# A 64-state scan whose odd states hold the channels' halves exchanged: y summed in four 64x64 tiles, carries copied on GpSimd

## Chip, cores and metric

One NeuronCore of a Trainium2 chip runs the whole program. The metric is device time in microseconds (us), here of one core, lower is better. The time of the kernel before is the median of three runs, 10685.8 us (10685.3 to 10687.49).

## What is computed

Four layers in a row on x of shape (4, 128, 64, 64): a sparse attention, a selective scan with 64 states, a rank-one attention, and a two-way scan with 16 states. The change touches the second layer alone. Cut to what matters, with L = 4096 positions per sample and C = 128 channels:

```python
xproj = xp @ W_in
x_mamba, x_conv = split(xproj, 2, axis=-1)
xc = depthwise_conv3x3(x_conv) + b_conv;  xc = xc * silu(xc)
u = layernorm(x_mamba) * gamma + beta
A = -exp(A_log)                                  # (C, 64)
dtbc = u @ W_dt + b_dt                           # 8 + 64 + 64 columns: dt, B, C
delta = softplus(dt_raw @ W_dtr + b_dtr)         # (b, L, C)
deltaA = exp(delta[..., None] * A)               # (b, L, C, 64)
dBu = delta[..., None] * B_ssm[:, :, None, :] * u[..., None]
h[l] = deltaA[l] * h[l - 1] + dBu[l]             # along L, for each channel and state
y = einsum('bldn,bln->bld', h, C_ssm) + u * D_param
out = (y + xc) @ W_out
return x + out
```

## The kernel before

`scan_layer` (L455) keeps channels on the 128 partitions and positions on the free axis. The 4 x 4096 positions are cut into NCH = 16 chunks of CH = 1024, numbered K, four to a sample. In each chunk it goes through the 64 states as 32 pairs, k = 0 to 31; a state of a chunk is a unit, and P = 32 K + k counts pairs. Each engine runs its own program, written out by hand in the order of the pairs, and they meet in semaphores.

For one pair P with its units 2P (even) and 2P + 1 (odd):

- ScalarE: `decays` (L824) writes exp(A delta) of a unit into one of 4 buffers; `odd_input` (L832) writes the transposed input of the odd unit, eight 128x128 pieces scaled by B, into `xt` (L842). It also does the softplus (`soft_exp`, `soft_log`), the copies out of PSUM, and SiLU.
- TensorE: `turn_back` (L672) transposes `xt` into the two PSUM banks of the odd input. `broadcast_B` (L661) writes the row of B of the next pair's even unit to all partitions, into the two banks of the even input. `add_state` (L682) adds h C of one unit to `y_sum`, two banks in which all 64 states of a chunk are accumulated, by matmuls with the 128x128 identity (L688). Between them stand the taps of the 3x3 convolution (`CONV`, L710: k = 3, 7, 14 to 20 and 23 to 31) and the preparation of the next chunk (`prep_*`), and the output projection of the chunk before (`project`, k = 21 and 22).
- VectorE: `scan` (L1038) runs the recurrence of 1024 positions, L1049, for the even and then the odd unit; `even_input` (L1031) multiplies du by the broadcast B in PSUM, L1036; `keep` (L1052) copies the last column of each unit's h into `carry` (L1055), in the three of four chunks whose state is carried on. Extra work: `add_y` at k = 0 (L1023), `gate_conv` at k = 1 and 21 (L1017), `rstds` and `newton` at k = 4, `scale_u` at k = 5 and 6 (L1005), `bt_copy` at k = 13, `residual` at k = 21 and 22 (L1029).
- GpSimd: `product` (L948) multiplies h by the broadcast row of C, L951, into `hc`. Extra instructions: `squares` at k = 1, `add_conv` at k = 2, `split_rest` at 12, `split_last` at 15, `soft_low`, `soft_max`, `soft_sum`, `input_rate` at 18, 19, 20, 21.
- SP: `load_row` (L544) loads one row of C, 4 KB, to all partitions of one of CS = 5 buffers of `hc`, once `sum_mm` says that the unit five before has been added.

The order of TensorE's work around the change, for pair P (L711 to L742):

```python
turn_back(P)
if P:
    add_state(2 * P - 2)
...                      # convolution, preparation, projection
if P + 1 < NCH * PAIRS:
    broadcast_B(P + 1, p if k + 1 < PAIRS else 1 - p)
if P:
    add_state(2 * P - 1)
```

and of VectorE's: `scan(P, 0)`, `scan(P, 1)`, then `even_input(P + 1)`, then the two `keep`, then any extra work. An even scan waits until its buffer of h is free: until the product of the unit four before is done.

Of the kernel before, what the change touches and what calls it, by code (L numbers as in the profile page):

```python
# [454 lines left out]
def scan_layer(nc, x, w, sel, weights_in, conv_weights):  # L455
# [13 lines left out]
    with ctx:  # L469
# [12 lines left out]
        delta = sb("delta", [128, 2, CH])  # L482
        du = sb("du", [128, 2, CH])
# [7 lines left out]
        part = sb("part", [PARTS * SEL, CH], BF16)  # L491
        z1, z2 = sb("z1", [128, CH]), sb("z2", [128, CH])
        z3, rows_sb = usq, z1[0:S1, :]
        carry = sb("carry", [128, S1])
# [27 lines left out]
        c_in = [sem(f"c_in_{i}") for i in range(CS)]  # L522
        hc_done = sem("hc_done"); sum_mm = sem("sum_mm"); y_out = sem("y_out"); yg_ready = sem("yg_ready")
# [15 lines left out]
        def _(sp):  # L539
# [11 lines left out]

            sp.dma_start(conv_raw, conv_weights).then_inc(conv_in, 16)
            store_rows(0)
            for K in range(NCH):
                for q in range(S1):
                    load_row(K, q)
                    if q == 26 and K + 1 < NCH:
                        store_rows(K + 1)

        @block.tensor  # L560
        def _(pe):
# [120 lines left out]
            def add_state(unit):  # L682
                K, q = divmod(unit, S1)
                if q == 0:
                    at_least(pe, y_out, K)
                pe.wait_ge(hc_done, unit + 1)
                for j in range(2):
                    ins = nc.tensor.matmul(y_sum[:, half(j)], ident, hc[:, unit % CS, half(j)], start=q == 0,  # L688
                                           stop=q == S1 - 1)
                ins.then_inc(sum_mm, 1)  # L690
# [20 lines left out]
            for K in range(NCH):  # L711
                p = K % 2
                for k in range(PAIRS):
                    P = K * PAIRS + k
                    turn_back(P)
                    if P:
                        add_state(2 * P - 2)
# [19 lines left out]
                    if k in (21, 22) and K:  # L737
                        project(K - 1, k - 21)
                    if P + 1 < NCH * PAIRS:
                        broadcast_B(P + 1, p if k + 1 < PAIRS else 1 - p)  # L740
                    if P:
                        add_state(2 * P - 1)  # L742
            for unit in range(NCH * S1 - 2, NCH * S1):
                add_state(unit)
# [4 lines left out]
        def _(act):  # L749
# [25 lines left out]
            def split_high(K):  # L775
                act.wait_ge(bdt_out, 2 * K + 2)
                nc.scalar.activation(part[:], rest[0:PARTS * SEL, :], ACT.Identity,
                                     scale=w[0:PARTS * SEL, L1_AT["below_top"]][:, 0:1]).then_inc(part_ready, 1)

            def split_middle(K):  # L780
                act.wait_ge(rest_ready, K + 1)
                nc.scalar.activation(part[:], rest[0:PARTS * SEL, :], ACT.Identity,
# [22 lines left out]
            def soft_log(K):  # L805
# [3 lines left out]
                nc.scalar.activation(z3[:], z3[:], ACT.Identity, bias=wt("minus_one")).then_inc(exp_ln, 1)  # L809
                nc.scalar.activation(z2[:], z1[:], ACT.Ln, bias=1.0).then_inc(exp_ln, 1)  # L810

            def duT_copy(K, p, j):
                act.wait_ge(duT_mm, 2 * K + j + 1)
                nc.scalar.activation(duT[:, p, 4 * j:4 * j + 4, :].rearrange("p t d -> p (t d)"), prep_ps,
                                     ACT.Identity).then_inc(duT_out, 1)
# [94 lines left out]
        def _(pool):  # L910
# [5 lines left out]
            def split_rest(K):  # L916
                pool.wait_ge(part_ready, 2 * K + 1)
                own = rest[0:PARTS * SEL, :]
                nc.gpsimd.tensor_tensor(own, own, part[:], ALU.subtract).then_inc(rest_ready, 1)

            def split_last(K, p):
                pool.wait_ge(part_ready, 2 * K + 2)
                nc.gpsimd.tensor_tensor(stack[:, p, :], rest[0:PARTS * SEL, :], part[:],
# [63 lines left out]
        def _(dve):  # L987
# [64 lines left out]
            def keep(unit):  # L1052
                q = unit % S1
                dve.wait_ge(scan_done, unit + 1)
# [1112 lines left out]
```

## Time and profile before

| | us |
|---|---|
| median of 3 runs | 10685.8 |
| the profiled execution, its own time | 10684.37 |
| its span, first to last instruction | 10682.6 |
| granted clock of TensorE over the span | 0.987 |

A row of a group names the line, the engine (PE = TensorE matmul, PEld = its weight load, DVE = VectorE, ACT = ScalarE, POOL = GpSimd), the operation, the tiles written and read, the shapes and the count; then busy us and mean ns of one; then the engine's idle time before such instructions and who ended it. A row of a timeline has the start in us from the span's start, the length in us, and neighbours of one line merged (x4 is four records); in brackets the idle time before. An fp32 matmul leaves two records. The ends of matmul records are modelled, so steps between starts are the better measure. "128*64" is the array's share in use, rows by columns.

### The profile page before, as it was taken

The numbers are of one execution on the slowest core, as the hardware profiler recorded it, in microseconds if no ns is written. First come the engines' busy times: TensorE is split into PE (matmuls) and PEld (weight loads), VectorE is DVE, ScalarE is ACT, GpSimd is POOL, SyncE is SP. The second block draws the span as 40 slices with busy tenths as digits, with TensorE's granted clock in tenths as the row PEclk, the third lists the DMA queues.
The fourth block names the chain that finished last, engine by engine and source line by source line (L and its number), as shares of the span: only waits on it lengthen the run. The fifth ranks groups of instructions, "written<-read, shape, count | busy, mean of one in ns | idle before, by whom it ended". The sixth has DMA issues, their size and how long they took to land. (4 is left out here: it accounts for less than half of the span.)

```text
span 10682.6 us, 128608 instructions
## 1 busy us (share of the span) xinstructions
PE 10171.5 (95%) x41860; PEld 5735.0 (54%) x41860; DVE 8525.5 (80%) x8102; ACT 8064.2 (75%) x14637; POOL 5901.9 (55%) x2628
## 2 busy tenths in 40 slices
PE   9999999999899999999999999989999999999996
PEld 6767767677444444444444444444444444444442
DVE  7858768588599999999999311179999999999997
ACT  5646646466588888888888555589999998888885
POOL 0000000000388888888888200068888888888885
PEclk9999999999899999999999999999999999999998
DMA  1000000000245555555555100045545555455555
GB/s 40 0 1 0 0 0 0 0 0 0 74 175 173 177 175 173 175 176 174 174 174 179 39 8 8 8 146 173 170 168 170 169 171 173 170 176 174 170 176 213
DMA packets 325682, 1207.45 MB, mean 113 GB/s; under 512 B 36624, under 2 KB 36752, under 8 KB 321552
## 3 DMA queue, kind: packets, MB, share of 16 engines
q1 hardware_dynamic: 325232, 1201.95, 32.9%
q8 instruction: 222, 3.64, 0.1%
q14 instruction: 228, 1.87, 0.1%
HBM read 1145.18 MB, written 56.62 MB: 113 GB/s over the span
## 5 line engine op out<-in xcount | busy, mean ns | idle before, releaser
L1816 POOL TENSOR_TENSOR l_ring<-l_ring 128x1024 f32<-128x1024 f32 x1024 | 2425.9, 2394 | 427.3 <-DVE l_ring L1894 425.7
L951 POOL TENSOR_TENSOR l_hc<-l_h,l_hc 128x1024 f32<-128x1024 f32 x1024 | 2398.9, 2365 | 451.5 <-DVE l_h L1049 450.9
L1894 DVE TENSOR_TENSOR_SCAN l_ring<-l_ring,l_carry,l_ps 128x1024 f32<-128x1024 f32 x960 | 2199.2, 2332 | 0.9
L1525 PE MATMUL l_ps<-l_ring,w_sb 128*128 128x512 f32 x4096 | 1960.5, 601 | 106.3 <-POOL l_ring L1816 74.1
L688 PE MATMUL l_ps<-l_hc,w_sb 128*128 128x512 f32 x4096 | 1936.5, 595 | 69.0 <-POOL l_hc L951 61.6
L1049 DVE TENSOR_TENSOR_SCAN l_h<-l_decay,l_carry,l_ps 128x1024 f32<-128x1024 f32 x768 | 1760.0, 2333 | 4.3 <-issue 0.4
L116 POOL COPY l_qm<-l_q 128x128 f32 x128 | 82.9, 649 | 2574.4 <-PE l_ps L188 2178.3
L829 ACT ACTIVATE l_decay<-l_delta,w_sb 128x1024 f32<-128x1024 f32 x1024 | 1152.7, 1138 | 168.6 <-DVE l_h L1049 168.4
L1706 ACT ACTIVATE l_xt<-l_duT,l_BT 128x128 f32<-128x128 f32 x4096 | 1246.0, 388 | 0.0
L842 ACT ACTIVATE l_xt<-l_duT,l_BT 128x128 f32<-128x128 f32 x4096 | 1245.9, 387 | 0.0
L1693 ACT ACTIVATE l_ring<-l_delta,w_sb 128x1024 f32<-128x1024 f32 x1024 | 1163.0, 1139 | 48.8 <-DVE l_ring L1894 47.7
L1525 PEld LDWEIGHTS l_ps<-l_ring,w_sb 128*128 128x128 f32 x4096 | 738.2, 190 | 733.1 <-issue 496.7
L212 PE MATMUL l_ps<-l_attnT,l_vT 128*128 128x128 f32 x8192 | 1095.7, 277 | 1.3 <-ACT l_attnT L283 1.3
L688 PEld LDWEIGHTS l_ps<-l_hc,w_sb 128*128 128x128 f32 x4096 | 735.3, 190 | 659.4 <-issue 491.8
L212 PEld LDWEIGHTS l_ps<-l_attnT,l_vT 128*128 128x128 f32 x8192 | 1013.9, 192 | 138.0 <-issue 114.7
L188 PE MATMUL l_ps<-l_k,l_qm 128*128 128x512 f32 x2048 | 1055.2, 599 | 16.9 <-DVE l_E L395 16.9
L1184 PE MATMUL l_ps<-l_E,l_hs 128*128 128x512 f32 x2048 | 880.0, 592 | 5.2 <-DVE l_hs L1250 5.2
L401 DVE SCALAR_TENSOR_TENSOR l_E<-l_relu,l_E 128x1024 f32<-128x1024 f32 x512 | 626.5, 1224 | 287.3 <-ACT l_E L276 287.3
L276 ACT ACTIVATE l_E<-l_E,l_offsets 128x1024 f32<-128x1024 f32 x512 | 587.0, 1147 | 291.2 <-DVE l_E L395 291.2
L270 ACT ACTIVATE l_relu<-l_ps,l_offsets 128x1024 f32<-128x1024 f32 x512 | 570.8, 1115 | 271.3 <-PE l_ps L188 269.5
L1211 ACT ACTIVATE l_E<-l_g,l_neg_max,l_f 128x4096 f32<-128x4096 f32 x128 | 486.4, 3800 | 378.8 <-PE l_ps L1184 366.9
L1878 DVE TENSOR_TENSOR l_ps<-l_du,l_ps 128x1024 f32<-128x1024 f32 x512 | 623.5, 1218 | 157.0 <-PE l_ps L1505 156.6
(232 smaller groups left out, 14528.8 us busy)
## 6 DMA issues: line engine op xcount, KB each, us to landing
l_hc<-l_rows_dram SPq DMA_DIRECT2D x1024, 512.0 KB, 3.6
l_ring<-l_rows_dram SPq DMA_DIRECT2D x1024, 512.0 KB, 3.7
l_gate_dram<-l_gate SPq DMA_DIRECT2D x32, 512.0 KB, 5.3
l_recon_dram<-l_recon SPq DMA_DIRECT2D x32, 512.0 KB, 5.4
l_gate<-l_gate_dram SPq DMA_DIRECT2D x32, 512.0 KB, 5.3
l_xw<-x_dram SPq DMA_DIRECT2D x30, 513.5 KB, 5.3
x_dram<-x SPq DMA_DIRECT2D x16, 512.0 KB, 2.6
l_loaded<-l_recon_dram SPq DMA_DIRECT2D x16, 512.0 KB, 4.9
```

The source lines that it names most:

```text
L188: ins = nc.tensor.matmul(logits[c % 2][:, j * BANK:(j + 1) * BANK], qm[:, h, :], k[:, c * CH + j * BANK:c * CH + (j + 1) * BANK], start=Tr ...
L212: ins = nc.tensor.matmul(ps[:, bank, 0:128], vT[:, t * 128:(t + 1) * 128], attnT[:, g % 2, j * 128:(j + 1) * 128], start=t == 0, stop=t == ...
L688: ins = nc.tensor.matmul(y_sum[:, half(j)], ident, hc[:, unit % CS, half(j)], start=q == 0, stop=q == S1 - 1)
L829: nc.scalar.activation(decay[:, unit % DS, :], delta[:, p, :], ACT.Exp, scale=wt("A")[:, q:q + 1]).then_inc(decay_ready, 1)
L842: ins = nc.scalar.activation(xt[:, (2 * P + hf) % XS, t * 128:(t + 1) * 128], duT[:, p, blk, :], ACT.Identity, scale=BT[:, p, blk, k:k + 1])
L951: nc.gpsimd.tensor_tensor(hc[:, unit % CS, :], h[:, unit % HS, :], hc[:, unit % CS, :], ALU.mult).then_inc(hc_done, 1)
L1049: nc.vector.tensor_tensor_scan(h[:, unit % HS, :], decay[:, unit % DS, :], odd_in if odd else even_in, before, ALU.mult, ALU.add).then_inc ...
L1525: ins = nc.tensor.matmul(y_sum[:, half(j)], ident, hc[:, unit % CS, half(j)], start=q == 0, stop=q == S3 - 1)
L1693: nc.scalar.activation(decay[:, unit % DS, :], delta[:, S % 2, :], ACT.Exp, scale=col("A", S % TI * S3 + q)).then_inc(decay_ready, 1)
L1706: ins = nc.scalar.activation(xt[:, (2 * P + hf) % XS, t * 128:(t + 1) * 128], duT[:, S % 2, 4 * hf + t, :], ACT.Identity, scale=BT[:, K % ...
L1816: nc.gpsimd.tensor_tensor(hc[:, unit % CS, :], h[:, unit % HS, :], hc[:, unit % CS, :], ALU.mult).then_inc(hc_done, 1)
L1894: nc.vector.tensor_tensor_scan(h[:, unit % HS, order], decay[:, unit % DS, order], x_now[:, order], before, ALU.mult, ALU.add).then_inc(sc ...
```

## The change

1. Odd units hold channels 64 to 127 on partitions 0 to 63 and the reverse. For that `duT_copy` writes its halves exchanged, `A` has its odd columns rolled by 64, and `crossed`, a copy of delta with exchanged halves, is written by two DMAs a chunk (`cross_delta`) and read by the odd units' `decays`.
2. `add_state` becomes `add_pair`, called twice a pair: phase 0 behind the preparation and ahead of `broadcast_B`, phase 1 behind it. Each phase has four matmuls of 64x64 by 512 columns: the even unit's halves go to their own half of the partitions of y's banks, the odd unit's to the other, and the two halves of the array's rows write different banks. `sum_mm` goes up by 2 at the end of phase 1. Phase 0 waits for both products of the pair.
3. `keep` leaves VectorE; GpSimd copies the carry just ahead of each unit's product, before it waits for the row of C.
4. `part` moves into the space of `z2`, with waits for who reads it.

```diff
@@ SP
+            def cross_delta(K):
+                sp.wait_ge(delta_ready, K + 1)
+                at_least(sp, decay_ready, S1 * K)
+                for side in range(2):
+                    sp.dma_start(crossed[64 * side:64 * side + 64, :],
+                                 delta[64 - 64 * side:128 - 64 * side, K % 2, :]).then_inc(crossed_in, 16)
...
+            cross_delta(0)
             for K in range(NCH):
                 for q in range(S1):
                     load_row(K, q)
                     if q == 26 and K + 1 < NCH:
                         store_rows(K + 1)
+                    if q == 62 and K + 1 < NCH:
+                        cross_delta(K + 1)
@@ TensorE
-            def add_state(unit):
-                K, q = divmod(unit, S1)
-                if q == 0:
-                    at_least(pe, y_out, K)
-                pe.wait_ge(hc_done, unit + 1)
-                for j in range(2):
-                    ins = nc.tensor.matmul(y_sum[:, half(j)], ident, hc[:, unit % CS, half(j)], start=q == 0,
-                                           stop=q == S1 - 1)
-                ins.then_inc(sum_mm, 1)
+            def add_pair(P, phase):
+                K, k = divmod(P, PAIRS)
+                if phase == 0:
+                    if k == 0:
+                        at_least(pe, y_out, K)
+                    pe.wait_ge(hc_done, 2 * P + 2)
+                    at_least(pe, sum_mm, 2 * P)
+                else:
+                    pe.wait_ge(first_half_mm, P + 1)
+                lower, upper = slice(0, 64), slice(64, 128)
+                for own, other, j in ((lower, upper, phase), (upper, lower, 1 - phase)):
+                    for odd, to in enumerate((own, other)):
+                        ins = nc.tensor.matmul(ps[to, 4 + j, :], ident[own, own], hc[own, (2 * P + odd) % CS, half(j)],
+                                               start=k == 0 and phase == 0, stop=k == PAIRS - 1 and phase == 1)
+                if phase == 1:
+                    ins.then_inc(sum_mm, 2)
+                else:
+                    ins.then_inc(first_half_mm, 1)
...
                     turn_back(P)
-                    if P:
-                        add_state(2 * P - 2)
                     if k in CONV:
                         convolution(K, *CONV[k])
...
+                    if P:
+                        add_pair(P - 1, 0)
                     if P + 1 < NCH * PAIRS:
                         broadcast_B(P + 1, p if k + 1 < PAIRS else 1 - p)
                     if P:
-                        add_state(2 * P - 1)
-            for unit in range(NCH * S1 - 2, NCH * S1):
-                add_state(unit)
+                        add_pair(P - 1, 1)
+            for phase in range(2):
+                add_pair(NCH * PAIRS - 1, phase)
@@ ScalarE
             def duT_copy(K, p, j):
                 act.wait_ge(duT_mm, 2 * K + j + 1)
-                nc.scalar.activation(duT[:, p, 4 * j:4 * j + 4, :].rearrange("p t d -> p (t d)"), prep_ps,
-                                     ACT.Identity).then_inc(duT_out, 1)
+                nc.scalar.activation(duT[:, p, 4 * j:4 * j + 4, :].rearrange("p t (s d) -> p t s d", s=2)[:, :, ::-1, :],
+                                     prep_ps.rearrange("p (t s d) -> p t s d", t=4, s=2), ACT.Identity).then_inc(duT_out, 1)
...
+                if q == 1:
+                    act.wait_ge(crossed_in, 32 * K + 32)
                 at_least(act, scan_done, unit - DS + 1)
-                nc.scalar.activation(decay[:, unit % DS, :], delta[:, p, :], ACT.Exp,
+                nc.scalar.activation(decay[:, unit % DS, :], crossed[:] if q % 2 else delta[:, p, :], ACT.Exp,
                                      scale=wt("A")[:, q:q + 1]).then_inc(decay_ready, 1)
@@ GpSimd
             def product(unit):
+                K, q = divmod(unit, S1)
+                pool.wait_ge(scan_done, unit + 1)
+                if K % NC < NC - 1:
+                    nc.gpsimd.tensor_copy(carry[:, q:q + 1], h[:, unit % HS, CH - 1:CH]).then_inc(kept, 1)
                 pool.wait_ge(c_in[unit % CS], 16 * (unit // CS) + 16)
-                pool.wait_ge(scan_done, unit + 1)
@@ VectorE
-            def keep(unit):
-                q = unit % S1
-                dve.wait_ge(scan_done, unit + 1)
-                nc.vector.tensor_copy(carry[:, q:q + 1], h[:, unit % HS, CH - 1:CH]).then_inc(kept, 1)
...
-                    if K % NC < NC - 1:
-                        keep(2 * P)
-                        keep(2 * P + 1)
```

Left out of the diff: the new declarations, `part` as a slice of `z2` with one wait in `split_high` (for `low_ready`) and one in `soft_log` (for `stack_ready`), and the rolled odd columns of `A`.

## Rows read from the trace of the kernel before

**Rows 1.** The page, part 1: each engine's busy time, share of the span and instructions.

```profile
PE 10171.5 (95%) x41860; PEld 5735.0 (54%) x41860; DVE 8525.5 (80%) x8102; ACT 8064.2 (75%) x14637; POOL 5901.9 (55%) x2628
```

**Rows 2.** Windows: us, then busy PE, PEld, DVE, ACT, POOL; clock, DMA share, GB/s.

```profile
2837.00:5939.00 3102.00, 2967.71 (x10923) 1526.29 (x10923) 3045.83 (x2499) 2625.39 (x5543) 2655.81 (x1144) 1.00 0.51 174
2780.00:2837.00 57.00, 28.43 (x72) 15.03 (x72) 5.33 (x11) 17.71 (x25) 15.45 (x7) 0.50 0.14 51
```

**Rows 3.** Groups of VectorE in 2837 to 5939: busy us, mean ns, idle before, releaser.

```profile
L1036 DVE TENSOR_TENSOR l_ps<-l_du,l_ps 128x1024 f32<-128x1024 f32 x511 | 618.8, 1211 | 26.9 <-PE l_ps L668 25.3
...
L1055 DVE COPY l_carry<-l_h 128x1 f32<-128x1 f32 x768 | 78.7, 146 | 0.0
...
L1023 DVE SCALAR_TENSOR_TENSOR l_yg<-l_u,w_sb,l_ps 128x1024 f32<-128x1024 f32 x15 | 19.2, 1281 | 11.4 <-PE l_ps L688 11.4
```

**Rows 4.** Timeline of VectorE, quiet pairs of chunks 7 and 8: start us, us, instruction.

```profile
4253.42 1.21 DVE L1036 TENSOR_TENSOR l_ps<-l_du,l_ps 128x1024 f32<-128x1024 f32 x1
4254.66 4.59 DVE L1049 TENSOR_TENSOR_SCAN l_h<-l_decay,l_carry,l_ps 128x1024 f32<-128x1024 f32 x2
...
4441.99 1.20 DVE L1036 TENSOR_TENSOR l_ps<-l_du,l_ps 128x1024 f32<-128x1024 f32 x1
4443.11 0.20 DVE L1055 COPY l_carry<-l_h 128x1 f32<-128x1 f32 x2
4443.23 4.58 DVE L1049 TENSOR_TENSOR_SCAN l_h<-l_decay,l_zero,l_ps 128x1024 f32<-128x1024 f32 x2
```

**Rows 5.** GpSimd's small instructions: L116's durations min/median/max, then a group with mean ns.

```profile
L116 POOL COPY l_qm<-l_q x128: 291/540/4265, 21.7 to 2657.2; 128x128 f32 x128
...
L2160 POOL MEMSET const-float32-1.0<- 128x1 f32 x1 | 0.1, 99 | 0.0
```

**Rows 6.** Timeline of TensorE, k = 10 of chunk 7 and k = 8 of chunk 8.

```profile
4260.23 1.88 PE L688 MATMUL l_ps<-l_hc,w_sb 128*128 128x512 f32 x4
4262.04 1.07 PE L601 MATMUL l_ps<-l_u,w_sb 128*64 128x512 f32 x2
4263.05 0.61 PE L668 MATMUL l_ps<-l_stack,sel 96*128 96x512 bf16 x2
...
4443.06 1.88 PE L688 MATMUL l_ps<-l_hc,w_sb 128*128 128x512 f32 x4
4444.78 1.02 PE L593 MATMUL l_ps<-l_u,w_sb 128*104 128x512 f32 x2
4445.63 0.60 PE L668 MATMUL l_ps<-l_stack,sel 96*128 96x512 bf16 x2
```

**Rows 7.** Timeline of TensorE in the first layer, two column tiles, then two row tiles.

```profile
27.70 3.65 PE L146 MATMUL l_ps<-l_q,w_sb 128*64 128x512 f32 x16
...
38.84 1.94 PE L161 MATMUL l_ps<-w_sb,l_E 64*128 64x128 f32 x24
```

**Rows 8.** Timeline of GpSimd, a quiet pair of chunk 7.

```profile
4251.41 4.69 POOL L951 TENSOR_TENSOR l_hc<-l_h,l_hc 128x1024 f32<-128x1024 f32 x2 [1.06 <-DVE l_h L1049]
```

**Rows 9.** Timeline of TensorE, then VectorE, k = 21 of chunk 6.

```profile
4131.97 1.98 PE L688 MATMUL l_ps<-l_hc,w_sb 128*128 128x512 f32 x4 [1.08 <-POOL l_hc L951]
...
4134.65 0.60 PE L668 MATMUL l_ps<-l_stack,sel 96*128 96x512 bf16 x2
...
4135.29 1.23 DVE L1036 TENSOR_TENSOR l_ps<-l_du,l_ps 128x1024 f32<-128x1024 f32 x1 [0.34 <-PE l_ps L668]
```

**Rows 10.** Timeline of GpSimd, chunk 6: from k = 2 on, then k = 19 and 20.

```profile
4025.95 9.29 POOL L951 TENSOR_TENSOR l_hc<-l_h,l_hc 128x1024 f32<-128x1024 f32 x4
...
4122.59 4.68 POOL L951 TENSOR_TENSOR l_hc<-l_h,l_hc 128x1024 f32<-128x1024 f32 x2
...
4129.56 4.67 POOL L951 TENSOR_TENSOR l_hc<-l_h,l_hc 128x1024 f32<-128x1024 f32 x2
```

**Rows 11.** Timeline of VectorE, scans of k = 3, chunk 6.

```profile
4022.12 4.59 DVE L1049 TENSOR_TENSOR_SCAN l_h<-l_decay,l_carry,l_ps 128x1024 f32<-128x1024 f32 x2
```

**Rows 12.** The page, part 6: issues of the rows of C, KB each, us to landing.

```profile
l_hc<-l_rows_dram SPq DMA_DIRECT2D x1024, 512.0 KB, 3.6
```

More of the change, by code:

```diff
@@ L482, in scan_layer @@
         delta = sb("delta", [128, 2, CH])
+        crossed = sb("crossed", [128, CH])
         du = sb("du", [128, 2, CH])
@@ L490, in scan_layer @@
         rest = sb("rest", [DT_AT + R1, CH])
-        part = sb("part", [PARTS * SEL, CH], BF16)
         z1, z2 = sb("z1", [128, CH]), sb("z2", [128, CH])
         z3, rows_sb = usq, z1[0:S1, :]
+        part = z2[0:PARTS * SEL, 0:CH // 2].bitcast(BF16)
         carry = sb("carry", [128, S1])
@@ L522, in scan_layer @@
         c_in = [sem(f"c_in_{i}") for i in range(CS)]
+        crossed_in = sem("crossed_in"); first_half_mm = sem("first_half_mm")
         hc_done = sem("hc_done"); sum_mm = sem("sum_mm"); y_out = sem("y_out"); yg_ready = sem("yg_ready")
@@ L776, in split_high @@
                 act.wait_ge(bdt_out, 2 * K + 2)
-                nc.scalar.activation(part[:], rest[0:PARTS * SEL, :], ACT.Identity,
+                at_least(act, low_ready, 2 * K)
+                nc.scalar.activation(part, rest[0:PARTS * SEL, :], ACT.Identity,
                                      scale=w[0:PARTS * SEL, L1_AT["below_top"]][:, 0:1]).then_inc(part_ready, 1)
@@ L781, in split_middle @@
                 act.wait_ge(rest_ready, K + 1)
-                nc.scalar.activation(part[:], rest[0:PARTS * SEL, :], ACT.Identity,
+                nc.scalar.activation(part, rest[0:PARTS * SEL, :], ACT.Identity,
                                      scale=w[0:PARTS * SEL, L1_AT["below_top"]][:, 1:2]).then_inc(part_ready, 1)
@@ L809, in soft_log @@
                 nc.scalar.activation(z3[:], z3[:], ACT.Identity, bias=wt("minus_one")).then_inc(exp_ln, 1)
+                act.wait_ge(stack_ready, K + 1)
                 nc.scalar.activation(z2[:], z1[:], ACT.Ln, bias=1.0).then_inc(exp_ln, 1)
@@ L918, in split_rest @@
                 own = rest[0:PARTS * SEL, :]
-                nc.gpsimd.tensor_tensor(own, own, part[:], ALU.subtract).then_inc(rest_ready, 1)
+                nc.gpsimd.tensor_tensor(own, own, part, ALU.subtract).then_inc(rest_ready, 1)
             def split_last(K, p):
                 pool.wait_ge(part_ready, 2 * K + 2)
-                nc.gpsimd.tensor_tensor(stack[:, p, :], rest[0:PARTS * SEL, :], part[:],
+                nc.gpsimd.tensor_tensor(stack[:, p, :], rest[0:PARTS * SEL, :], part,
                                         ALU.subtract).then_inc(stack_ready, 1)
@@ L2100, in layer1_arrays @@
                ("out_w", 0, W_out), ("ident", 0, _np.eye(128)), ("ones", 0, _np.ones((128, 1))),
-               ("A", 0, A_log[:, by_unit]), ("below_top", 0, below_top), ("minus_one", 0, _np.full((128, 1), -1)),
+               ("A", 0, _np.where(_np.arange(S1) % 2, _np.roll(A_log[:, by_unit], 64, 0), A_log[:, by_unit])),
+               ("below_top", 0, below_top), ("minus_one", 0, _np.full((128, 1), -1)),
                ("bdt_b", 0, column(_np.concatenate([b_dt[even_B]] * PARTS + [b_dt[:R1]]))),
```

## The prediction

> **What bounds the kernel now.** I read the page first: TensorE 95% busy, VectorE 80%, which would make TensorE the thing to relieve [rows 1]. But only the 64-state scan is touched, so the next view is its stretch alone: 3102 us, in which VectorE is busy for 3045.8 and TensorE for 2967.7, with the full clock granted [rows 2]. Both are nearly full, and the groups of VectorE say which ends last: its idle time is 26.9 us before L1036 and 11.4 us before L1023, almost all of it ended by TensorE, and the two copies of L1055 are 78.7 us of its work [rows 3]. So the tempting forecast is 79 + 37 us of gain. The timeline of VectorE decides the larger part. In a chunk without carry copies, the step from the start of L1036 to the start of the next scan is 4254.66 - 4253.42 = 1.24 us; in a chunk with them it is 4443.23 - 4441.99 = 1.24 us too, though the two copies start at 4443.11, between the two [rows 4]. The scan must wait for L1036 to end anyhow, and the copies lie in that gap. A quiet pair of states takes 1.24 + 4.59 less an overlap of 0.09, or 5.74 us, with or without them. No part of this change shortens that: 512 such pairs are VectorE's alone.
>
> **Part 1, carry copies leave VectorE.** Nothing in quiet pairs. Where another VectorE instruction stands behind the copies, the gap is used anyhow and they cost: the pair with k = 5 has a step of its own behind them. Two copies start to end take 0.20 us [rows 4]; I take 0.12 us a pair, in about 4 pairs a chunk where nothing else is late, over the 12 chunks that keep carries: -6 us. Their cover, if the gap went, would be worth 0.12 us in every pair.
>
> **Part 2, carry copies on GpSimd.** They stand ahead of each product, so the product ends later by the copy. No row shows a 128x1 GpSimd copy. From below: VectorE's second copy adds 0.06 us (0.20 for two, 0.146 for one) [rows 3, 4]. From above: GpSimd's 128x128 copy takes at least 0.29 us, median 0.54 with VectorE in its way; nearest in size is its 128x1 memset, 0.10 us [rows 5]. I take c = 0.10 a copy and keep 0.06 to 0.29.
>
> **Part 3, y's sums on TensorE.** Before, a pair needs four 128x512 matmuls, each two records; four records take 4444.78 - 4443.06 = 1.72 us, so a pair 3.44 us [rows 6]. After, there are eight 64x64 matmuls, in two phases of four. Do tiles run side by side in fp32? Sixteen records of two column tiles (L146) take 3.65 us, where sixteen in a row at 0.43 would take 6.9; 24 records of two row tiles (L161) take 1.94 us [rows 7]. I take four at a time: a phase is two passes, 0.86 us. Changing the tile shape costs: four records before a 64-column matmul take 4262.04 - 4260.23 = 1.81 us instead of 1.72, and that matmul with the way back 1.01 instead of 0.85 (L593) [rows 6]. So a phase is 0.86 + 0.20 = 1.06 us, two are 2.12, and TensorE gains 1.3 us a pair.
> The Trainium skill, TensorEngine Tiling (Array Packing), section Tiling Modes, speaks against switching back and forth: a change of mode drains the array. It gives no price; if the whole tail of a matmul stood open each way, some 0.07 us more each, the sum would be about 6 us higher (an estimate). Of the trace, the L601 rows show a drain of about 0.1 us, and I stay with them.
> What is it worth? At most what VectorE waits for TensorE: 25.3 + 11.4 us [rows 3], plus 0.08 us at each of some 62 waits, since the instruction before it overlaps the next by that much: -42 us.
>
> **Part 4, the new wait.** A phase sums both states of a pair, so it waits for the second product, and broadcast_B of the next pair is queued behind phase 0; L1036 waits for broadcast_B. In a quiet pair the two products end at 4251.41 + 4.69 = 4256.10, 2.60 us after the scan's end (4253.50, 0.08 behind the start of L1036 [rows 4, 8]). Then 0.06 of wait, 1.06 of phase 0 and 0.64 from the start of the broadcast to L1036 (4135.29 - 4134.65) [rows 9] make 1.76. L1036 is due 5.66 after the scan's end. The spare is 5.66 - 2.60 - 1.76 = 1.30 us, less 2c: 1.10. Convolution and preparation stand ahead of phase 0 and fit in the wait for the product. Before, TensorE waited only for the pair's first product there, 2.3 us earlier.
> GpSimd is not always on time. From k = 18 to 21 it has an extra instruction per pair, and its pair takes 4129.56 - 4122.59 = 6.97 us [rows 10], so it falls back 1.22 us a pair; with copies, 1.22 + 0.20 = 1.42. Four pairs: 5.68; VectorE's own extra work there (L1017 and two L1029) takes 1.85 of it, the spare 1.10; 2.7 us of stall are left. At k = 1 and 2 the same happens once: the second product of k = 3 ends at 4025.95 + 4.65 = 4030.60, 3.9 us after the scan's end at 4026.71 [rows 10, 11]; the copies of three pairs and VectorE's shorter pairs make it 4.7, and 4.7 + 1.76 - 5.66 = 0.8 us. Newton's steps behind it, 0.2; the extra instruction at k = 15, 0.1. Together 3.8 us a chunk, times 12: +46. In three chunks without copies: 4 x 1.22 - 1.30 - 1.85 = 1.7, +5 in all.
>
> **Part 5, the rest.** The exchanged copy of delta is two more DMAs of 256 KB a chunk; a 512 KB load lands in 3.6 us [rows 12]. It is issued late in k = 30, lands in k = 31, and its first reader is due 4 us later: nothing on the path. If it came later than that, the two chunk-end pairs would stretch by the difference. Loads of C rows are now freed in twos, at the end of phase 1; landing 3.6 us later, about 2 us ahead of their product. part in z2, and the permuted write of duT, wait for things long done. ScalarE stands at the delta copy's wait for about 3 us, its next exponentials and L842 behind it, and is ahead of VectorE by more than that. After the last product both phases follow instead of one unit's sum: +1.
>
> **Sum.** -6 - 42 + 46 + 5 + 1 = +4 us. The profiled execution took 10684.4 us (span 10682.6), 1.4 under the median of the runs, 10685.8. So 10688 by the terms; I say 10690. What a measurement of this kernel can tell from no change is about 0.2%, 21 us. With c = 0.06 it is 10 us less; with 0.29 each chunk stalls 5 us more, 10751.
>
> **Rivals.**
> Faster. GpSimd's copy is nearly free and VectorE catches up in the bursts, so that most of the 42 us remain: about 10655. For it: copies behind each other overlap on VectorE (0.06), and every term of part 4 is an estimate of small differences. Against it: the bursts stall VectorE already before, 0.34 us at 4135.29 [rows 9], with more tolerance than after.
> Slower. The copy on GpSimd is dear. Place: the burst at k = 18 to 21 and every pair after an extra. Each 0.1 us of c adds some 2.7 us a chunk, 33 us in all; from c = 0.15 on, the sum passes +21 us. At 0.29, 10751. For it: the 128x128 copy's 0.29 to 0.54. Against: the memset.
> The array takes two tiles at a time, not four: a phase is 1.72 + 0.20 = 1.92 us. TensorE's work is 2967.7 / 512 = 5.80 us a pair on average [rows 2]; it becomes 5.80 - 3.44 + 3.84 = 6.20 against VectorE's 5.8, 0.4 us more in 512 pairs: about 10880. No row shows a tiling in both directions at once; rows show each alone.
> The clock. In the setup stretch TensorE was busy for half of the time and had 0.50 granted, its 1.2 GHz level; in the scan 1.00, 2.4 GHz [rows 2]. After, TensorE works 5.80 - 1.3 = 4.5 us a pair on average, less in quiet ones, and in a burst it stands still behind the product. At the lower level it would need 9.0 us a pair, 3.2 more than VectorE's: 512 pairs, 12330. Against it: 4.5 of 5.8 us is still far more than the half of the setup. The Trainium skill, TensorE: Matmul & The Clock Gate, Part 1, says that an idle array is throttled; the trace agrees for the setup stretch.
> That the change does not do what it says has no room: each instruction moved is in the diff.
>
> **How the numbers follow.** Forecast case, both sides of zero: 0.50; dear copy 0.20; faster 0.20; two tiles 0.07; clock 0.03. The forecast's own range is 10665 to 10720. The likeliest gives the time, 10690. The range leaves out two tiles and clock (0.10) and the far ends of the others: 10650 to 10760. The forecast case lies within 21 us in 0.35 of its 0.50, below in 0.07, above in 0.08; of the faster case 0.18 counts as faster; of the dear copy 0.15 as slower. Faster 0.27, same 0.40, slower 0.33.
>
> **What would show it.** L1055 gone from VectorE and the step from L1036 to the scan still 1.24 us (if it shrinks, I misread the cover). Matmuls of the sum start in fours, a phase about 1.06 us. Idle of VectorE before L1023 near zero, but before L1036 about 50 us, in k = 4 and 20 to 24, where TensorE had waited for the second product. GpSimd's copies near 0.1 us. Pairs away from the bursts at 5.74 us. A quiet pair under 5.7 us, or a stall in most pairs, would make the whole account wrong.

## The result, and the profile after

The changed kernel takes 10704.4 us, median of 20 runs, beside 10686.3 us of the kernel before in 20 runs: ratio 1.0017, 95% interval 1.001 to 1.0024. It is 18 us slower, inside the 21 us that were called no change. (One run of the kernel before, 21317 us, is not in the ratio.) The profiled execution has a span of 10700.9 us, against 10682.6.

The page, part 1 and the granted clock of part 2, of the changed kernel:

```profile
PE 9693.9 (91%) x45956; PEld 5162.6 (48%) x45956; DVE 8497.7 (79%) x7334; ACT 8071.1 (75%) x14637; POOL 5998.8 (56%) x3396
...
PEclk9999999999899999999999999999999999999998
```

TensorE gave up 478 us of busy time [rows 1], and the kernel is not faster for it. GpSimd has 97 us more. All of it happened in the scan stretch, so the next view is the windows; the columns are named in the first line, and the last line is the whole stretch:

```profile
core 0: us, PE busy (x) PEld busy (x) DVE busy (x) ACT busy (x) POOL busy (x), PEclk, DMA share, GB/s
4100.70:4104.10 3.40, 3.40 (x17) 1.69 (x17) 3.37 (x3) 3.40 (x10) 3.15 (x3) 0.56 0.02 5
4158.80:4162.20 3.40, 3.40 (x17) 1.86 (x10) 3.31 (x3) 1.19 (x2) 2.89 (x4) 0.57 0.29 70
2838.00:5956.00 3118.00, 2491.19 (x15010) 953.76 (x15010) 3020.89 (x1732) 2632.48 (x5544) 2751.44 (x1912) 0.96 0.53 177
```

TensorE is busy for 2491 us where it was 2968 [rows 2]; VectorE for 3021 of 3118, where it was 3046 of 3102. Its work fell by 25 us and its idle time rose by 41. The clock is 0.96, not 1.00; the first two lines are two of its gaps, and we return to them. The groups of VectorE in that stretch, and below them the line of its waits for the broadcast (us in total, times, longest):

```profile
L1065 DVE TENSOR_TENSOR l_ps<-l_du,l_ps 128x1024 f32<-128x1024 f32 x512 | 620.3, 1212 | 93.6 <-PE l_ps L680 93.5
...
L1052 DVE SCALAR_TENSOR_TENSOR l_yg<-l_u,w_sb,l_ps 128x1024 f32<-128x1024 f32 x15 | 18.8, 1255 | 0.0
L1023 DVE TENSOR_TENSOR l_tmp<-l_var,l_root 128x8 f32<-128x8 f32 x15 | 8.5, 567 | 8.3 <-ACT l_root L782 8.3
...
L1025 DVE TENSOR_TENSOR l_tmp<-l_tmp,l_root 128x8 f32<-128x8 f32 x15 | 2.5, 167 | 1.1
```

```profile
DVE l_ps L1065 <- PE l_ps L680: 93.5, 80, 24.6
```

The copies are gone, and so is the wait before add_y (L1052, 11.4 us in [rows 3]). But even_input (L1065) now waits 93.5 us, of which 24.6 is one wait ahead of the first pair, outside the window of before: 68.9 us in 79 waits, where it was 25.3 in 47 [rows 3]. Newton's first step (L1023) takes 567 ns on average, its equal in form beside it (L1025) 167. In the kernel before the first step took 796 (the line stands at experiment 2), so by itself it became shorter.

A quiet pair, k = 8 and 9 of chunk 6, on VectorE, GpSimd and TensorE in turn:

```profile
4071.91 1.21 DVE L1065 TENSOR_TENSOR l_ps<-l_du,l_ps 128x1024 f32<-128x1024 f32 x1
4073.15 4.58 DVE L1078 TENSOR_TENSOR_SCAN l_h<-l_decay,l_carry,l_ps 128x1024 f32<-128x1024 f32 x2
```

```profile
4069.82 0.19 POOL L978 COPY l_carry<-l_h 128x1 f32<-128x1 f32 x1 [0.79 <-DVE l_h L1078]
4069.95 2.37 POOL L980 TENSOR_TENSOR l_hc<-l_h,l_hc 128x1024 f32<-128x1024 f32 x1
4072.28 0.18 POOL L978 COPY l_carry<-l_h 128x1 f32<-128x1 f32 x1
4072.41 2.36 POOL L980 TENSOR_TENSOR l_hc<-l_h,l_hc 128x1024 f32<-128x1024 f32 x1
```

```profile
4069.08 1.09 PE L707 MATMUL l_ps<-l_hc,w_sb 64*64 64x512 f32 x8 [0.83 <-POOL l_hc L980]
4070.10 0.60 PE L680 MATMUL l_ps<-l_stack,sel 96*128 96x512 bf16 x2
4070.63 1.09 PE L707 MATMUL l_ps<-l_hc,w_sb 64*64 64x512 f32 x8
```

The step from the start of even_input to the start of the scan is 4073.15 - 4071.91 = 1.24 us, as in [rows 4], now without any copy in it. On GpSimd a copy's record lasts 0.19 us, but the product starts 0.13 after it, and from product to product it is 4072.41 - 4069.95 = 2.46 us, where two products without copies took 4.69 from start to end [rows 8], a step of some 2.32. A phase of the sum takes 4070.10 - 4069.08 = 1.02 us up to the broadcast; the broadcast takes 4070.63 - 4070.10 = 0.53. In the kernel before, the sum started 4446.08 - 4445.63 = 0.45 us behind the broadcast of [rows 6]:

```profile
4446.08 1.45 PE L688 MATMUL l_ps<-l_hc,w_sb 128*128 128x512 f32 x3
```

The burst of GpSimd in the same chunk, from k = 18 on: GpSimd, TensorE, VectorE:

```profile
4130.27 2.39 POOL L980 TENSOR_TENSOR l_hc<-l_h,l_hc 128x1024 f32<-128x1024 f32 x1
...
4137.47 2.39 POOL L980 TENSOR_TENSOR l_hc<-l_h,l_hc 128x1024 f32<-128x1024 f32 x1
...
4139.92 2.36 POOL L980 TENSOR_TENSOR l_hc<-l_h,l_hc 128x1024 f32<-128x1024 f32 x1
4142.22 2.38 POOL L962 TENSOR_TENSOR l_delta<-l_delta,l_usq 128x1024 f32<-128x1024 f32 x1
```

```profile
4142.33 1.09 PE L707 MATMUL l_ps<-l_hc,w_sb 64*64 64x512 f32 x8 [2.67 <-POOL l_hc L980]
4143.35 0.60 PE L680 MATMUL l_ps<-l_stack,sel 96*128 96x512 bf16 x2
```

```profile
4136.80 1.23 DVE L1065 TENSOR_TENSOR l_ps<-l_du,l_ps 128x1024 f32<-128x1024 f32 x1 [0.21 <-PE l_ps L680]
...
4144.00 1.23 DVE L1065 TENSOR_TENSOR l_ps<-l_du,l_ps 128x1024 f32<-128x1024 f32 x1 [1.35 <-PE l_ps L680]
...
4151.19 1.23 DVE L1065 TENSOR_TENSOR l_ps<-l_du,l_ps 128x1024 f32<-128x1024 f32 x1 [0.22 <-PE l_ps L680]
...
4158.39 1.23 DVE L1065 TENSOR_TENSOR l_ps<-l_du,l_ps 128x1024 f32<-128x1024 f32 x1 [0.88 <-PE l_ps L680]
```

From one pair's first product to the next it is 4137.47 - 4130.27 = 7.20 us, where it was 6.97 [rows 10]. The second product of the pair starts at 4139.92 and ends at 4142.28; the sum starts at 4142.33, the broadcast at 4143.35, even_input at 4144.00, after 1.35 us of idle time. The four waits here are 0.21 + 1.35 + 0.22 + 0.88 = 2.7 us. (The average over the eleven chunks of the table below is 2.9.)

To place the loss in the chunk, I took the distance from the start of each even scan to the start of the next pair's, less 5.745 us, and averaged it over the eleven chunks from 1 to 14 that keep their carries. The pairs that differ most are shown; kernels 1 to 11 are the experiments below, named by what they do. VectorE's own extra work is part of each number.

```
excess over 5.745 us, in pair    k=0   k=4   k=14  k=15  k=20  k=21  k=22  k=23  k=24
before                           2.08  2.49  -0.01 0.78  0.00  1.69  0.58  0.59  0.00
after                            1.19  3.50  0.13  0.61  0.31  2.59  0.79  1.24  0.03
1 copies back on VectorE         1.19  2.70  -0.01 0.00  0.02  2.29  0.58  0.78  0.06
2 before, copies on GpSimd       2.07  3.44  0.21  0.97  0.00  2.11  0.78  0.98  0.00
3 sum behind the broadcast       1.19  3.36  -0.01 0.00  0.00  1.12  0.62  0.12  2.23
4 full-array sums                2.56  3.97  0.85  1.06  1.10  2.57  0.78  0.98  0.00
5 filling matmul                 1.19  3.45  -0.01 0.47  0.33  2.61  0.77  0.98  0.11
6 1 and 3 together               1.19  2.40  -0.01 0.00  0.00  1.25  0.58  -0.01 0.24
7 Newton in PSUM                 1.19  3.17  0.01  0.07  0.33  2.51  0.97  1.21  0.02
8 1, 3 and 7 together            1.31  1.72  -0.01 0.00  0.00  1.25  0.58  0.11  0.47
9 before, order of 3, and 7      3.13  1.74  -0.01 0.21  0.00  1.25  0.58  -0.01 0.00
10 experiment 8 and filling      1.58  1.78  -0.01 0.00  0.00  1.25  0.58  0.01  0.13
11 before, with 7                2.08  1.90  -0.01 0.77  0.00  1.69  0.58  0.59  0.00
```

Between before and after: 0.9 us won at k = 0 (add_y waits for nothing), 1.0 lost at k = 4, and 2.1 between k = 20 and 23. Of the pairs not shown, k = 1, 5, 6 and 13 won 0.12 us each and k = 25 and 27 won 0.13, k = 17 lost 0.03, and the other 16 are the same to 0.01 us.

### The profile page after: what moved, and what is told of

Read it like the earlier page. It is cut to its first block and busy times, and to the rows that moved or that the text cites. A ratio compares the mean times of both kernels' runs of the same rounds, so it can differ in the third digit from the quotient of the medians.

```text
span 10700.9 us, 136605 instructions
## 1 busy us (share of the span) xinstructions
PE 9693.9 (91%) x45956; PEld 5162.6 (48%) x45956; DVE 8497.7 (79%) x7334; ACT 8071.1 (75%) x14637; POOL 5998.8 (56%) x3396
## 5 line engine op out<-in xcount | busy, mean ns | idle before, releaser
L707 PE MATMUL l_ps<-l_hc,w_sb 64*64 64x512 f32 x8192 | 1183.7, 650 | 428.6 <-POOL l_hc L980 426.4
L116 POOL COPY l_qm<-l_q 128x128 f32 x128 | 82.2, 644 | 2576.2 <-PE l_ps L188 2180.6
L855 ACT ACTIVATE l_decay<-l_delta,w_sb 128x1024 f32<-128x1024 f32 x512 | 585.5, 1144 | 297.4 <-DVE l_h L1078 296.5
L690 PEld LDWEIGHTS l_ps<-w_sb,l_xt 128*128 128x128 f32 x4096 | 458.8, 145 | 628.1 <-DVE l_h L1078 512.6
```

Source lines behind the costliest of these rows:

```text
L707: ins = nc.tensor.matmul(ps[to, 4 + j, :], ident[own, own], hc[own, (2 * P + odd) % CS, half(j)], start=k == 0 and phase == 0, stop=k == P ...
```

## The experiments

Medians are of 5 or more runs of each kernel (4 of kernel 4), beside 21 to 27 runs of the kernel before in the same session, whose medians were 10684.1 to 10685.5; the changed kernel's 10704.4 stood beside 10686.3. Differences between kernels of different sessions are therefore good to about 2 us.

**1. The carry copies back on VectorE.** Behind even_input, as before; the rest as changed.

```diff
 def product(unit):
-                if K % NC < NC - 1:
-                    nc.gpsimd.tensor_copy(carry[:, q:q + 1], h[:, unit % HS, CH - 1:CH]).then_inc(kept, 1)
...
+                    if K % NC < NC - 1:
+                        keep(2 * P)
+                        keep(2 * P + 1)
```

> The changed kernel with the carry copies back on VectorE, behind even_input. Theory A (the burst account): the copies cost by making GpSimd later. In the changed kernel's trace the pairs of a chunk that keeps carries exceed 5.745 us by 12.2 us in sum, those of a chunk without copies by 9.75; with the copies in VectorE's gap a chunk should come to 9.75 plus 0.12 us at some five pairs, 10.35: 1.85 us less in 12 chunks, 22 us, so about 10682, the time of the kernel before. Rival B (the two-unit wait and the clock of TensorE make the loss, the copies are innocent): within 6 us of the changed kernel, 10698 to 10710.

10676.4 us, ratio 0.9992 (0.9983 to 1.0001): 28 us below the changed kernel, which is 6 more than the theory's 22 and far from the rival. Tiles, order and delta's copy together, without the copies on GpSimd, are 9 us faster than before. Newton's first step, in VectorE's groups:

```profile
L1021 DVE TENSOR_TENSOR l_tmp<-l_var,l_root 128x8 f32<-128x8 f32 x15 | 6.9, 461 | 8.3 <-ACT l_root L782 8.3
```

It falls from 567 to 461 ns: the copies reach this far, too.

**2. The copies on GpSimd alone.** The kernel before, with nothing but this.

```diff
 def product(unit):
+                K, q = divmod(unit, S1)
+                pool.wait_ge(scan_done, unit + 1)
+                if K % NC < NC - 1:
+                    nc.gpsimd.tensor_copy(carry[:, q:q + 1], h[:, unit % HS, CH - 1:CH]).then_inc(kept, 1)
                 pool.wait_ge(c_in[unit % CS], 16 * (unit // CS) + 16)
-                pool.wait_ge(scan_done, unit + 1)
...
-                    if K % NC < NC - 1:
-                        keep(2 * P)
-                        keep(2 * P + 1)
```

> The kernel before with nothing but the carry copies moved to GpSimd. Theory A: TensorE waits only for the first product here, so the later products fall into its larger tolerance: VectorE wins 0.12 us at some five pairs of 12 chunks (-6 us), the burst at k = 18 to 21 falls back up to 0.96 us more (at most +11 us): 10680 to 10692. Rival (copies on GpSimd cost wherever they stand): 10705 or more.

10706.4 us, ratio 1.002 (1.0011 to 1.0029): 21 us slower than before, and my theory's sum for it was wrong; the rival's number stands. VectorE's groups, and last Newton's first step in the kernel before:

```profile
L1039 DVE TENSOR_TENSOR l_ps<-l_du,l_ps 128x1024 f32<-128x1024 f32 x512 | 620.8, 1212 | 75.0 <-PE l_ps L668 72.8
...
L997 DVE TENSOR_TENSOR l_tmp<-l_var,l_root 128x8 f32<-128x8 f32 x15 | 17.3, 1156 | 8.6 <-ACT l_root L760 8.6
```

```profile
L994 DVE TENSOR_TENSOR l_tmp<-l_var,l_root 128x8 f32<-128x8 f32 x15 | 11.9, 796 | 8.6 <-ACT l_root L760 8.6
```

Of the 72.8 us, 24.6 are again the wait ahead of the first pair; 48.3 are left, in 69 waits, where it was 25.3 [rows 3]. Newton's first step takes 1156 ns where it took 796. The table says where the rest went: 0.95 us at k = 4, 0.2 each at k = 14 and 15, 1.0 from k = 21 to 23. That the wait for two products was needed to make late products dear was an error: from k = 1 on GpSimd works without a pause up to k = 4, eight copies of 0.12 us make its product there end 0.96 us later (in chunk 5), and Newton waits for exactly that.

**3. The sum behind the broadcast.** Both phases behind broadcast_B, except at k = 0, where add_y is due.

```diff
-                    if P:
+                    if k == 0 and P:
                         add_pair(P - 1, 0)
                     if P + 1 < NCH * PAIRS:
                         broadcast_B(P + 1, p if k + 1 < PAIRS else 1 - p)
+                    if k:
+                        add_pair(P - 1, 0)
                     if P:
                         add_pair(P - 1, 1)
```

> The changed kernel with both phases of the sum behind broadcast_B, except at k = 0. Theory A: broadcast_B no longer waits for the second product; the stalls before even_input at k = 3, 14 and 20 to 24 go (some 4.7 us a chunk in 12 chunks, 1.3 in three), and what is left of the burst, about 0.9 us a chunk, comes from turn_back, which now stands behind the wait: 10650 to 10660. Rival B (GpSimd's burst stalls the scan wherever the wait stands, or the clock of TensorE does): 10690 to 10710.

10676.6 us, ratio 0.9993 (0.9984 to 1.0002): 28 us better than the changed kernel, but not the 45 to 55 expected. Its waits of VectorE and Newton's first step:

```profile
DVE l_h L1080 <- PE l_ps L690: 34.5, 25, 2.7
...
L1025 DVE TENSOR_TENSOR l_tmp<-l_var,l_root 128x8 f32<-128x8 f32 x15 | 26.5, 1765 | 8.3 <-ACT l_root L784 8.3
```

The broadcast is late nowhere after the first pair. Two stalls took its place: turn_back, now behind the wait, makes the odd scan wait 34.5 us in 25 waits (2.23 us at k = 24 in the table, where I had allowed 0.9), and Newton's step at k = 4 is at 1765 ns: the earlier VectorE gets there, the longer it stands.

**4. Full-array sums.** Each phase as two 128x128 matmuls. The odd unit's halves are added to the wrong channels of y.

```diff
-                lower, upper = slice(0, 64), slice(64, 128)
-                for own, other, j in ((lower, upper, phase), (upper, lower, 1 - phase)):
-                    for odd, to in enumerate((own, other)):
-                        ins = nc.tensor.matmul(ps[to, 4 + j, :], ident[own, own], hc[own, (2 * P + odd) % CS, half(j)],
-                                               start=k == 0 and phase == 0, stop=k == PAIRS - 1 and phase == 1)
+                for odd in range(2):
+                    ins = nc.tensor.matmul(ps[:, 4 + phase, :], ident, hc[:, (2 * P + odd) % CS, half(phase)],
+                                           start=k == 0 and odd == 0, stop=k == PAIRS - 1 and odd == 1)
```

> The changed kernel with each phase done by two full-array matmuls (128x128 identity) in place of four 64x64: y's odd half goes to the wrong channels, the output is not the reference's. A phase is 1.72 us in place of 1.06, without changes of the tile shape. Theory A: the spare behind the second product falls from 1.06 to 0.4 us, and TensorE has 5.8 us of work a pair again: each of the five late places a chunk grows by 0.66 us, and pairs with a convolution are late too: 10760 to 10830. Rival (the tiles are worth nothing, the wait is all): within 15 us of the changed kernel.

10769.2 us, ratio 1.0077 (1.0062 to 1.0093): 65 us slower than with tiles, as the theory had it. The tiles do their work; the kernel spends what they earn. Its waits of VectorE:

```profile
DVE l_ps L1063 <- PE l_ps L680: 114.2, 116, 3.0
DVE l_yg L1050 <- PE l_ps L705: 19.3, 15, 2.1
```

**5. A filling matmul.** One more fp32 matmul a pair, zeros times u, into y's first bank.

```diff
                     turn_back(P)
+                    if k > 1:
+                        nc.tensor.matmul(ps[:, 4, :], zero[:, 0:1].broadcast_to([128, 128]), u[:, p, half(0)],
+                                         start=False, stop=False)
```

> The changed kernel with one more fp32 matmul a pair on TensorE from k = 2 on, behind turn_back: a zero matrix times u, added to y's first bank, two records, 0.86 us, in the time in which TensorE waits for the product. The changed kernel's trace has 58 stretches of the scan, 232 us in sum, at the 0.50 clock; the kernel before has none. Clock theory: the stretches go or become few, the stall at k = 15 (0.6 us more than the account gives) and part of those at k = 21 to 24 go: 10690 to 10698. Rival (the half clock costs nothing, since the waits hide it, or a zero matrix does not hold the clock): 10702 to 10712, with the stretches gone or still there.

10697.4 us, ratio 1.001 (1.0001 to 1.0019): 7 us faster with more work. The stretches at the low clock in the scan, counted from 2850 us on, went from 58 to 17, 232 to 61 us. Up to 5890 us, the same window in the changed kernel and in this one (columns as above):

```profile
2838.00:5890.00 3052.00, 2439.58 (x14704) 935.52 (x14704) 2955.70 (x1696) 2582.24 (x5441) 2698.76 (x1889) 0.96 0.53 177
```

```profile
2838.00:5890.00 3052.00, 2751.55 (x15672) 1086.73 (x15671) 2965.85 (x1699) 2588.55 (x5447) 2705.94 (x1892) 0.99 0.54 177
```

What such a stretch does is seen in the changed kernel at k = 14 and 15 of chunk 6, the first of the two windows above, at 0.56 of the clock. TensorE, then VectorE:

```profile
4100.80 1.99 PE L707 MATMUL l_ps<-l_hc,w_sb 64*64 64x512 f32 x8
4102.71 1.55 PE L690 MATMUL l_ps<-w_sb,l_xt 128*128 128x128 f32 x8
...
4107.65 1.09 PE L707 MATMUL l_ps<-l_hc,w_sb 64*64 64x512 f32 x8
4108.67 1.09 PE L690 MATMUL l_ps<-w_sb,l_xt 128*128 128x128 f32 x8
```

```profile
4107.76 1.23 DVE L1065 TENSOR_TENSOR l_ps<-l_du,l_ps 128x1024 f32<-128x1024 f32 x1 [1.01 <-PE l_ps L680]
```

The phase of the sum behind the broadcast takes 4102.71 - 4100.80 = 1.91 us against 4108.67 - 4107.65 = 1.02 a pair later, and turn_back 1.39 instead of 0.93; the next broadcast is late by 1.01 us. That stall is 0.74 us at k = 14 and 15 on average, where the prediction had 0.1 for the extra instruction at k = 15.

That it comes from the clock can be seen inside the changed kernel, chunk by chunk. Seven of the eleven chunks (2, 4, 6, 8, 10, 12, 14) have a stretch at the low clock at k = 14 and 15, and lose 1.05 to 1.25 us in these two pairs. The other four (1, 5, 9, 13) have none there and lose nothing; instead a stretch covers 2.9 to 3.2 us of their k = 23, where they lose 1.65 to 1.83 us against 0.97 to 0.99 in the seven, which have at most 1.7 us of it there. In sum the low clock costs these chunks about 11 us (an estimate: 7 times 1.16 and 4 times 0.72). The filling matmul gave back 7 of them, because it has a price of its own: in experiment 5 no stretch falls on k = 15 in any of the eleven chunks, and each still loses 0.39 to 0.52 us there, 5 us in sum.

**6. Experiments 1 and 3 together.**

> The changed kernel with the carry copies back on VectorE and both phases behind broadcast_B except at k = 0. With the copies alone put back it took 10676.4, its pairs k = 20 to 24 exceed 5.745 us by 3.7 us in sum; the chunks without copies of the kernel with the sum behind exceed by 2.65 there. If the two remedies act on the same stall: 15 us less than 10676, 10655 to 10668. Rival (the wait before turn_back eats it): 10672 to 10682.

10649.5 us, ratio 0.9967 (0.9955 to 0.9979): 27 us below either, better than expected (six runs, one of them at 10662.3). Without the copies GpSimd's burst is shorter, and turn_back's wait at k = 24 shrinks from 2.23 to 0.24 us.

**7. Newton's intermediates in PSUM**, on the changed kernel, so that no step has two operands in SBUF.

```diff
+                nc.vector.tensor_scalar(prep_ps[:, 2 * BLK:3 * BLK], prep_ps[:, 0:BLK], 1.0 / C, 1e-5, ALU.mult, ALU.add)
+                dve.drain()
...
+                tmp_ps = prep_ps[:, BLK:2 * BLK]
-                nc.vector.tensor_tensor(tmp[:], var[:], root[:], ALU.mult)
+                nc.vector.tensor_tensor(tmp_ps, prep_ps[:, 2 * BLK:3 * BLK], root[:], ALU.mult)
...
-                nc.vector.tensor_tensor(tmp[:], tmp[:], root[:], ALU.mult)
+                nc.vector.tensor_tensor(tmp_ps, tmp_ps, root[:], ALU.mult)
```

> The changed kernel with Newton's steps (k = 4) reading and writing their small intermediates in PSUM, so that each has at most one operand in SBUF; one more VectorE instruction of about 0.16 us in the wait for ScalarE's root. Theory: the first of them (mean 567 ns against 167 of its neighbours, 796 before) stands until GpSimd's running product ends, and this, not the broadcast, carries most of what k = 4 lost (3.50 us over 5.745, 2.49 before; 3.44 where only the copies moved, 3.36 where the sum went behind the broadcast). Then k = 4 falls to 2.3 to 2.9 us and the time by 0.6 to 1.2 us a chunk: 10686 to 10696. Rival (the length of that instruction has another cause): k = 4 stays at 3.5, 10702 to 10708.

10690.0 us, ratio 1.0005 (0.9996 to 1.0014): 14 us below the changed kernel. Chunk 6 at k = 4, first the changed kernel's VectorE and GpSimd, then this kernel's VectorE:

```profile
4041.72 0.90 DVE L1023 TENSOR_TENSOR l_tmp<-l_var,l_root 128x8 f32<-128x8 f32 x1 [0.55 <-ACT l_root L782]
4042.69 0.17 DVE L1025 TENSOR_TENSOR l_tmp<-l_tmp,l_root 128x8 f32<-128x8 f32 x1
```

```profile
4040.21 2.38 POOL L980 TENSOR_TENSOR l_hc<-l_h,l_hc 128x1024 f32<-128x1024 f32 x1
```

```profile
4034.86 0.16 DVE L1020 TENSOR_SCALAR l_ps<-l_ps 128x8 f32<-128x8 f32 x1
4035.49 0.17 DVE L1026 TENSOR_TENSOR l_ps<-l_ps,l_root 128x8 f32<-128x8 f32 x1 [0.47 <-ACT l_root L782]
4035.74 0.17 DVE L1028 TENSOR_TENSOR l_ps<-l_ps,l_root 128x8 f32<-128x8 f32 x1
...
4036.24 0.16 DVE L1032 TENSOR_TENSOR l_rstd<-l_root,l_ps 128x8 f32<-128x8 f32 x1
```

In the changed kernel the step started at 4041.72 and ended at 4042.62, the moment at which GpSimd's product (4040.21 + 2.38 = 4042.59) ended. Now it takes 0.17. In the table k = 4 falls by 0.33 only (I expected 0.6 to 1.2), since the broadcast is late there as well; in chunks without copies it falls from 2.61 to 1.77. The rest of the 14 us is at k = 14 and 15 (0.74 to 0.08), where a stretch of low clock fell in one of the eleven chunks instead of seven. Why fewer fell there is not explained by the edit.

**8. Experiments 1, 3 and 7 together.**

> All three together: carry copies on VectorE, both phases behind broadcast_B except at k = 0, Newton's intermediates in PSUM. If all act: another 0.6 us a chunk below the kernel with the first two, 10645 to 10660, the fastest so far. If Newton's length has another cause: the same as that kernel.

10642.8 us, ratio 0.9958 (0.9945 to 0.9972): faster than both kernels and just below the range. Newton's share is 7 us. What is left of its waits for turn_back:

```profile
DVE l_h L1081 <- PE l_ps L690: 14.4, 14, 2.3
```

**9. The same order without tiles.** The kernel before with both add_state behind the broadcast and Newton's edit (the diff of 7, and this one).

```diff
-                    if P:
+                    if k == 0 and P:
                         add_state(2 * P - 2)
...
                         broadcast_B(P + 1, p if k + 1 < PAIRS else 1 - p)
+                    if k:
+                        add_state(2 * P - 2)
                     if P:
                         add_state(2 * P - 1)
```

> The kernel before, with its full-array sums, no exchanged halves and no new copies, but with both add_state behind broadcast_B (except at k = 0) and Newton's intermediates in PSUM. It asks what the tiles themselves are worth once the order is mended. Tiles matter: TensorE has 5.8 us of work a pair, two sums of 1.72 us behind broadcast_B push turn_back 1.6 us into the next pair and convolution pairs catch up slowly, so y's sum at the chunk's end is late by a us or more and some 1 us a chunk more is lost: 10660 to 10675, 20 to 30 us behind the best kernel (10642.8). Rival (the order did it all): 10640 to 10655.

10675.8 us, ratio 0.9992 (0.9983 to 1.0001), 0.8 above the first range: without tiles the order gives nothing (experiment 11 has the same time). With it, the tiles, and the exchange that they need, are worth 33 us. The full-array sums are late where y is due, at k = 0 (3.13 us in the table):

```profile
DVE l_yg L1028 <- PE l_ps L688: 26.6, 15, 1.8
```

**10. Experiment 8 with the filling matmul of 5.**

> The best kernel so far (carry copies on VectorE, both phases behind broadcast_B, Newton in PSUM; 10642.8) with the filling matmul behind turn_back. Its trace still has 46 stretches, 198 us, at the 0.50 clock. Clock theory: with most of them gone, the scattered stalls before the odd scan (15.1 us) shrink: 10632 to 10640. Rival (there the order hides the half clock, the filler only adds work): 10641 to 10650.

10635.6 us, ratio 0.9953 (0.994 to 0.9967), 7 us below experiment 8, the fastest of all, inside the first range. Between 2838 and 5890 us the mean clock is 0.99 where experiment 8 had 0.97, and turn_back's waits are 4.0 us in 5 where experiment 8 had 15.1 in 15:

```profile
DVE l_h L1084 <- PE l_ps L690: 4.0, 5, 1.3
```

**11. Newton's edit on the kernel before.**

> The kernel before with Newton's intermediates in PSUM alone. The first of Newton's steps falls from 796 to about 170 ns, 0.6 us in 15 chunks, 9 us: 10675 to 10679. Rival (something else sets k = 4 there, the ScalarE root or TensorE): 10683 to 10687.

10675.3 us, ratio 0.9992 (0.9983 to 1.0001): 9 us, as expected.

## Why the prediction was right, and where it was not

The forecast was 10690 us and no change; measured were 10704.4 and +0.17%. That the sum came near zero is a balance of gains and losses of some 45 us each, so part of the closeness is luck.

**What bounds the scan: right.** The cover of the copies (1.24 us with and without) and the pair of 5.74 us stand in the profile after, and 16 of 32 pairs are the same to 0.01 us.

**Part 1: right.** In pairs with a step behind the copies 0.12 us went (k = 1, 5, 6, 13).

**Part 2: the size was a little off.** c was taken as 0.10 us; a product is 0.13 later for its copy. By the prediction's rule (33 us for 0.1) that would be 10 us more, but no run shows these 10. With c = 0.10 the rule and part 1 charge the copies 33 - 6 = 27 us in all, and experiment 1 measures 28, of which 8 are the low-clock stall at k = 14 and 15.

**Part 3: the price right, the gain in part.** A phase was put at 1.06 us and measures 1.02 with another 0.08 in the broadcast; four tiles do run at a time, and full-array matmuls in their place cost 65 us. The gain of 42 us came in part: the 11.4 us before add_y came whole and k = 25 and 27 are free of their waits, but the wait at k = 15 turned into another.

**Part 4: the burst right, its neighbour incomplete.** For k = 20 to 24, 2.7 us of stall and 1.85 of VectorE's own work were forecast, 4.55 in all; the chunks with no stretch of low clock there (2, 10, 14) have 4.7, the average is 4.96. At k = 4, 0.8 for the late broadcast and 0.2 for Newton were forecast, and 1.0 was lost. The late broadcast is there, 1.09 us in chunk 6, and without Newton's stand it costs more than was forecast: 3.17 us at k = 4 in experiment 7 against 1.90 in experiment 11. But it is not the only reason: experiment 2 loses 0.95 there without any new wait, since Newton stands until GpSimd's running product ends, and all eight copies since k = 1 move that end. Either reason alone nearly makes the loss, and the sentence that puts Newton's steps at 0.2 us has the second one wrong. So the copies were charged to the new wait alone, and alone they cost 21 us.

**Part 5** held nearly: ScalarE waited for the exchanged copy of delta 14 times, at most 2.6 us, and VectorE never for ScalarE's exponentials. In the scan, loads of C rows landed 4.6 us after their issue instead of 3.6, and five products had to wait for their row, 7.7 us in sum; none did before.

**Rivals.** The dear copy, named as the slower side, is the mechanism by which the kernel is slower, though c is near its low end: without the copies it would be 9 us faster than before. Two tiles at a time is refuted. The clock was priced as all or nothing, at 0.03; it came in 58 short stretches and cost about 11 us by the comparison of chunks at experiment 5, most of the 14 that the forecast lacked. That case was missing, and the sum has the clock at nothing. A slip in the chances: the parts given for "faster" make 0.07 + 0.18 = 0.25, not 0.27.

## What to carry to other kernels

Before moving an instruction to another engine, see whether it costs anything where it is: of 79 us of copies all but some 6 were covered, and the move made them dear. An engine with slack on average can be late in bursts; ask what waits for its last product there, and put what must be early (here the broadcast) ahead of that wait. Relief of an engine pays only where the bound engine waits for it: the same tiles were worth 9 us in one order (experiment 1 beside the kernel before) and 33 us in another.

## What the runs showed of the hardware

**VectorE stands until GpSimd's instruction ends.** A 128x8 multiply with both operands in SBUF took 0.90 us, up to the end of a GpSimd product, and 1765 ns on average in experiment 3; with one of them in PSUM, 0.17 us. Of the 15 such steps in the changed kernel's scan, ten lasted 0.19 to 1.25 us, and each of them ended 21 to 25 ns after a GpSimd product; the other five ran while GpSimd was idle and took 0.17. The Trainium skill, SBUF — State Buffer, section SBUF: two separate sides, says that a VectorE instruction with two SBUF inputs and a GpSimd instruction that reads SBUF exclude each other for the whole instruction; the traces agree.

**TensorE's clock fell inside a busy loop.** Busy for 2491 of 3118 us, it was at the 1.2 GHz level for 232 us, in 58 stretches, and in the kernel before, busy for 2968 of 3102, never. Busy time alone does not tell: experiment 9, busy for 2924 of 3052, has eight such stretches. Filling work with a zero matrix brought the mean clock from 0.96 to 0.99. Before the two stretches shown above, the array had paused behind GpSimd's product for 0.99 us (k = 14) and 2.67 us (k = 23), and no pause shortly before any of the 58 was longer than 2.7 us. The Trainium skill, TensorE: Matmul & The Clock Gate, Part 1, tells of a throttle that idle time brings on; the trace agrees in so far as each pause shown stands ahead of a stretch, and shows that pauses this short can be enough. Which pause brings a stretch on, and which does not, no run here shows.

**fp32 tiles.** Eight 64x64 matmuls of 512 columns run four at a time: sixteen records in two phases of 1.02 us. No row of the kernel before had shown tiling in both directions at once.
